# Moving the second half projections to score step 7 and two VectorE steps by one maximum in a fused transformer block

## The chip, the cores and the metric

The kernel runs on one core of a Trainium2 chip. The metric is the device time of one execution in microseconds (us). The core's engines are TensorE (PE in the profile, with PEld for its weight loads), VectorE (DVE), ScalarE (ACT), GpSimd (POOL) and SyncE (SP), which here only issues transfers.

## The reference

The input is 32 samples of 512 tokens by 256 features. Each sample goes through half a feed-forward block, an attention block, and half a feed-forward block again:

```
x = x + 0.5 * ffn(layernorm(x), Wr, br, W1, b1, W2, b2)      # routed: 2 of 8 experts per sample, gelu
x = x + attention(layernorm(x), Wqkv, Wo)                    # 16 heads of 16, rotary q and k, causal softmax
x = x + 0.5 * ffn(layernorm(x), Wr, br, W1, b1, W2, b2)
```

Inside the attention, q and k are rotated (`q = cos * q + rotate_half(q) * sin`), the scores are `q @ k.T / 4` with a causal mask, and the softmax over them weights v. Everything is float32 in the reference; the kernel splits float32 values into a high and a low float16 part and multiplies the parts.

## The kernel before

Three phases follow each other: the first feed-forward over all samples, the attention over all samples, the second feed-forward. The change is in the attention.

**Slots.** Each sample has 16 heads in four groups g = 0 to 3 of four heads. The attention runs in slots, one for each sample s and group g, in this order on each engine. Within a slot TensorE runs eleven score steps n = 0 to 10 ("score step 7" of the change is n = 6, the seventh). A step of it does two things: `scores(s, g, n)` makes transposed scores for the group two slots back, and `max_scores(s, g, n)` makes scores of the present group, only so that their row maxima can be taken. VectorE reduces each of those in `maxima(s, g, n)`, ScalarE makes the exponentials (`exps`, L1073) from the first kind, GpSimd masks the diagonals (L912), and TensorE multiplies with v (`probs_v`, L1202).

**Work between the steps.** Other work is put behind the steps by hand. On TensorE: while g is 0 or 1 the q and k projections of the next sample in four tiles t, two a slot, each as two halves of three matmuls (`project_qk`, L1219), in slot 2 its v projections (`project_v`, L1233), the transposes of a group's output (`turn_output`, L1255), and in slot 3 the transposes of the sample after the next and the output projection (`transpose_o` L1271, `project_o` L1280). On VectorE: `begin_rope` (L974 and L975) multiplies a finished q or k tile by the cosines and swaps its pairs, `rope_low` (L981) makes the low float16 part of a rotated tile, `normalise_output` (L1016, L1020) divides by the softmax sums, and `layernorm_stats` (L107 to L119) makes the statistics of the sample after the next. GpSimd finishes the rotation in `rope` (L920, L924), which begins when VectorE has swapped the pairs.

**Waits.** The maxima use three banks in turn, so `max_scores` step n waits until the maximum of about two or three steps before has ended: the first step of a slot for the ninth maximum of the slot before, step n = 5 for maximum n = 2, step n = 6 for maximum n = 3, n = 10 for n = 7. The `scores` steps use two banks: step n waits for the exponential of step n - 2. `begin_rope(t)` waits for the second half of the projection of tile t; the fourth mask of a slot waits for the last exponential, and the second `rope` of a slot stands behind that mask on GpSimd. On VectorE and GpSimd `rope_low` reads two tensors in SBUF, as do both halves of `rope`; of the other VectorE steps of a slot, the maxima, `begin_rope` and `normalise_output` read PSUM and at most one tensor in SBUF.

A "sample" below is the stretch of slots 0 to 3 of one s; times in it are those of the sample that begins at 1108.09 us of the profiled execution.

Of the kernel before, what the change touches and what calls it, by code (L numbers as in the profile page):

```python
# [58 lines left out]
def wait(eng, sem, value):  # L59

    if isinstance(value, int) and value <= 0:
        return
    eng.wait_ge(sem, value)
# [690 lines left out]
def attention(nc, ctx, tab, mem, src, dst, cos, sin, first):  # L754
# [44 lines left out]
    def after_first(eng):  # L799

        for i in range(3):
            eng.wait_ge(first.stored[i], 16 * len(range(i, B, 3)))

    def group(G):
        return not isinstance(G, int) or 0 <= G < B * 4

    def sample(s):
        return not isinstance(s.b, int) or 0 <= s.b < B

    def of_group(s, g, lag):  # L810

        return s + (g - lag) // 4, (g - lag) % 4

    def half_of(g):

        return g // 2, GH * (g % 2)
# [145 lines left out]
    def vector(dve):  # L962
        def start():
            nc.vector.memset(v[0], 1.0).then_inc(consts_set, 1)
            dve.wait_ge(consts_set, 1)

        def begin_rope(n, t):
            idx = 4 * n.b + t
            dve.wait_ge(qk_done, idx + 1)
            if idx == 0:  # L970
                dve.wait_ge(tables_loaded, 32)

            wait(dve, rope_done, idx - 1)
            nc.vector.tensor_tensor(by_cos[t % 2][:], x_ps[t % 2][:], cos_t[:], ALU.mult)  # L974
            nc.vector.stream_shuffle(swapped[t % 2][:], x_ps[t % 2][:], [i ^ 1 for i in range(32)]).then_inc(rope_in, 1)  # L975

        def rope_low(n, t):
            dve.wait_ge(qk_hi, 4 * n.b + t + 1)

            wait(dve, q_written if t < 2 else k_written, 32 * n.b)  # L980
            nc.vector.tensor_tensor(qk.lo[:, t, :], rotated[t % 2][:], qk.hi[:, t, :], ALU.subtract).then_inc(qk_lo, 1)  # L981

        def maxima(s, g, n):
            G = 4 * s.b + g
            dve.wait_ge(mx_done, 11 * G + n + 1)
            if G == 0 and n == 0:
                dve.wait_ge(over_done, 1)
            if n == 0:

                wait(dve, mt_done, G - 1)  # L990
            bank = mx_ps[MX_BANK[n]]
            out = mx[g % 2]
            if n < 4:
                i = 3 - n // 4
                w = (i + 1) * P
                nc.vector.tensor_tensor_reduce(out=bank[:, 0:w], in0=bank[:, 0:w], in1=over[:, T - w:T], scale=1.0, scalar=LOWEST,  # L996
                                               op0=ALU.add, op1=ALU.max, accum_out=out[:, n % 4, i:i + 1]).then_inc(max_done, 1)
                return
            if n < 8:
                o_ap, i_ap = out[:, n - 4, 2:3], bank[:, 0:3 * P]  # L1000
            elif n < 10:
                a = 2 * (n - 8)
                o_ap, i_ap = out[:, a:a + 2, 1], bank[:].rearrange("p (a n) -> p a n", a=2)
            else:
                o_ap, i_ap = out[:, :, 0], bank[:].rearrange("p (a n) -> p a n", a=4)
            nc.vector.tensor_reduce(o_ap, i_ap, AX_X, ALU.max).then_inc(max_done, 1)  # L1006


        def normalise_output(s, g):

            G = 4 * s.b + g
            os, og = of_group(s, g, 3)
            half, j = half_of(og)
            turned = pv_ps[:].rearrange("p (i a d) -> p i a d", i=NT, a=GH)
            dve.wait_ge(o_turned, G - 2)
            nc.vector.reciprocal(inverse[:].rearrange("p (i a) -> p i a", i=NT), turned[:, :, :, DH]).then_inc(inverse_done, 1)  # L1016

            wait(dve, oT_done, NC * (os.b - 1))
            dve.wait_ge(inverse_done, G - 2)
            nc.vector.tensor_tensor(  # L1020
                on[os.par][:].rearrange("p i (j q d) -> p i j q d", q=2, d=DH)[:, :, j:j + GH, half, :],
                turned[:, :, :, 0:DH],
                inverse[:].rearrange("p (i a d) -> p i a d", i=NT, d=1).broadcast_to([P, NT, GH, DH]), ALU.mult).then_inc(on_done, 1)

        def low_of(lo, hi, n, c, hi_done, lo_done):
            dve.wait_ge(hi_done, NC * n.b + c + 1)
            nc.vector.tensor_tensor(lo[:, c, :], x_ps[c][:], hi[:, c, :], ALU.subtract).then_inc(lo_done, 1)

        def slot(s, g):
            G = 4 * s.b + g  # L1030
            if G == 1:
                after_first(dve)
                nc.vector.memset(v[1], 1.0).then_inc(consts_set, 1)
            for n in range(11):
                if group(G):
                    maxima(s, g, n)
                if g in (1, 2) and sample(s + 1) and n in (0, 3):
                    rope_low(s + 1, 2 * (g - 1) + (n == 3))
                if group(G - 3) and n == 5:
                    normalise_output(s, g)  # L1040
                if g < 2 and sample(s + 1) and n in (2, 6):
                    begin_rope(s + 1, 2 * g + (n == 6))
                if g == 2 and sample(s + 2) and n == 1:
                    dve.wait_ge(x_loaded, 16 * ((s + 2).b + 1))

                    wait(dve, xn_done, NT * (s + 2).b)
                    layernorm_stats(nc, dve, stats_step, stats_done, (s + 2).b, x, stats, pair, ve)
                if g == 3 and sample(s + 2) and n in (1, 2):
                    low_of(xT.lo, xT.hi, s + 2, n - 1, xT_hi, xT_lo)
                if g == 3 and sample(s + -1) and n in (5, 7):  # L1050
                    low_of(oT.lo, oT.hi, s + -1, int(n == 7), oT_hi, oT_lo)
                if g == 3 and sample(s + -1) and n == 10:
                    add_residual(s + -1, 0)
                if g == 0 and sample(s + -2) and n == 0:
                    add_residual(s + -2, 1)

        def add_residual(n, j):
            dve.wait_ge(res_loaded[n.par], 16 * (n.half + 1))
            dve.wait_ge(o_done, 2 * n.b + j + 1)
            r = res[n.par][:, 2 * j:2 * j + 2, :]  # L1060
            nc.vector.tensor_tensor(r, x_ps[j][:].rearrange("p (t d) -> p t d", t=2), r, ALU.add).then_inc(res_done, 1)

        at = Turns()
        at.start, at.slot = start, slot
        return at
# [64 lines left out]
    def tensor(pe):  # L1130
# [155 lines left out]
        def slot(s, g, between=None):  # L1286
            G = 4 * s.b + g
            cur, run = group(G), group(G - 2)
            if G == 0:
                pe.wait_ge(first.gelu_done, 8 * B)  # L1290
            if G == 2:
                pe.wait_ge(stacks_set, 32)
                pe.wait_ge(first.out_done, 2 * B)
            if G == 6:
                pe.wait_ge(stacks_set, 64)
            before = group(G - 3)
            for n in range(11):
                if between:
                    between(n)
                if run and n < 10:  # L1300
                    scores(s, g, n)
                if cur:
                    max_scores(s, g, n)
                if n == 2 and before:
                    probs_v(s, g, 3, 1, 1)
                if n == 1 and group(G - 1):
                    turn_maxima(s, g)
                if n == 2 and before:
                    probs_v(s, g, 3, 2, 3)
                    probs_v(s, g, 3, 3, 2)  # L1310
                if n == 5 and before:
                    turn_output(s, g)
                if g < 2 and sample(s + 1) and n in (0, 1, 4, 5):
                    project_qk(s + 1, 2 * g + (n > 3), half=(n in (1, 5)))
                if g == 2 and sample(s + 1) and n in (0, 1, 4, 5):
                    project_v(s + 1, (0, 1, 4, 5).index(n))
                if g == 3 and sample(s + 2) and n == 0:
                    transposes(s + 2)
                if run and n == 8:
                    probs_v(s, g, 2, 0, 0)  # L1320
                if g == 3 and sample(s + -1) and n == 4:
                    transpose_o(s + -1, s)
                if g == 3 and sample(s + -1) and n >= 9:
                    project_o(s + -1, 2 * (n - 9))
                    project_o(s + -1, 2 * (n - 9) + 1)
# [285 lines left out]
```

## Time and profile before

| what | value |
|---|---|
| time, median of 3 runs | 2299.27 us (2298.2 to 2305.56) |
| the profiled execution's own time | 2291.23 us |
| its span, first to last instruction | 2289.5 us |
| PE busy | 2109.5 us, 92% |
| DVE busy | 1931.8 us, 84% |
| ACT busy | 1354.4 us, 59% |
| POOL busy | 1306.6 us, 57% |
| mean granted TensorE clock | 0.989 of 2.4 GHz |

The shares are averages over the three phases. What a change to the attention is worth has to be read from its slots: which wait ends last there. A start in the time-ordered view is that of the instruction itself; the numbers in square brackets are the idle time of the engine before it and what ended that.

### The profile page before, as it was taken

The page shows a single profiled execution, that of the slowest core. Times are in us where ns is not written, and L with a number is a line of the kernel's source. Part 1 is how long each engine was busy: PE and PEld are TensorE (multiplying, and loading weights), DVE is VectorE, ACT ScalarE, POOL GpSimd, SP SyncE. Part 2 cuts the span into 40 slices and gives each one's busy share as a digit, 9 for nine tenths or more (in the row PEclk, how much of TensorE's full clock was granted, in tenths as well). Part 3 has the DMA queues.
Part 4 walks back from the last instruction along what each step waited for, and adds up shares of the span by engine and source line. Part 5 has one row for each costly group of instructions (what it writes and reads, how often), then busy time and mean ns, then how long its engine had stood idle before and what let it go on. Part 6 is the DMA issues. An engine that isn't in the chain of part 4 may idle for free.

```text
span 2289.5 us, 52899 instructions
## 1 busy us (share of the span) xinstructions
PE 2109.5 (92%) x17682; PEld 1141.4 (50%) x17682; DVE 1931.8 (84%) x4485; ACT 1354.4 (59%) x2568; POOL 1306.6 (57%) x1462
## 2 busy tenths in 40 slices
PE   4999999889999999999999999999999888999999
PEld 2666666434444444444444444444444434666666
DVE  6777788788999899999989998999999865777776
ACT  3455444266667666666666676666666655445553
POOL 6666667454555455456545554554555425666664
PEclk9999999899999999999999999999999999999999
DMA  6656666444445444444444454444445423666665
GB/s 208 192 192 207 201 203 200 116 89 89 98 95 101 94 94 98 89 94 93 99 89 100 95 101 94 96 92 96 93 94 98 99 70 118 197 202 194 204 207 167
DMA packets 280391, 295.29 MB, mean 129 GB/s; under 512 B 45784, under 2 KB 263224, under 8 KB 280120
## 3 DMA queue, kind: packets, MB, share of 16 engines
q1 hardware_dynamic: 280120, 291.90, 50.3%
q8 instruction: 143, 2.34, 0.5%
q14 instruction: 128, 1.05, 0.2%
HBM read 140.08 MB, written 83.89 MB: 98 GB/s over the span
## 4 chain that ended last, share of the span: by engine, by line
PE 45%; DVE 33%; SPq 7%; issue 6%; DMA 5%; ACT 4%; DVEq 0%; ACTq 0%
PE bank L710 8%; DVE bank L996 7%; DVE at_mx L1006 7%; PE bank L728 7%; PE bank L1185 6%; PE bank L1202 6%; PE bank L1219 4%; PE bank L1280 4%; ACT probs L1073 3%; DVE turned L975 3%; DVE v_qk L981 3%; DVE turned L974 2%; DVE at_stats L107 2%; PE bank L1255 2%; PE bank L1167 2%
## 5 line engine op out<-in xcount | busy, mean ns | idle before, releaser
L1073 ACT ACTIVATE probs<-bank 128x512 f32<-128x512 f32 x1280 | 747.0, 603 | 456.9 <-PE bank L1185 447.5
L912 POOL TENSOR_SCALAR_AFFINE_SELECT probs<-probs 128x512 f32<-128x512 f32 x512 | 320.4, 638 | 661.1 <-ACT probs L1073 659.3
L1006 DVE TENSOR_REDUCE at_mx<-bank 128x1 f32<-128x384 f32 (+2 forms) x896 | 509.6, 608 | 78.5 <-PE bank L1167 77.0
L1185 PE MATMUL bank<-stacks 49*128 49x512 f16 (+3 forms) x2048 | 458.7, 302 | 71.4 <-ACT probs L1073 71.0
L996 DVE CUSTOM_DVE_ANT_0 bank<-bank,xn 128x512 f32<-128x512 f32 x512 | 351.6, 698 | 38.8 <-PE bank L1158 36.2
L1185 PEld LDWEIGHTS bank<-stacks 49*128 49x128 f16 x2048 | 136.0, 94 | 458.6 <-ACT probs L1073 334.2
L1162 PE MATMUL bank<-stacks 48*128 48x384 f16 (+2 forms) x1536 | 307.7, 275 | 22.1 <-DVE at_mx L1006 15.6
L1167 PE MATMUL bank<-mask,turn 64*128 64x128 bf16 (+2 forms) x896 | 230.7, 257 | 0.0
L1158 PE MATMUL bank<-stacks 48*128 48x512 f16 x512 | 198.5, 389 | 10.6 <-DVE at_mx L996 6.4
L924 POOL TENSOR_TENSOR turned<-turned 128x512 f32<-128x512 f32 x128 | 184.7, 1443 | 19.1 <-POOL turned L920 0.4
L628 ACT ACTIVATE turned<-bank,b1s 128x512 f32<-128x512 f32 x128 | 88.2, 689 | 181.0 <-PE bank L710 179.3
L920 POOL TENSOR_TENSOR turned<-turned,at_sin 128x512 f32<-128x512 f32 x128 | 178.8, 1397 | 27.7 <-DVE turned L975 27.7
L628 ACT ACTIVATE probs<-bank,b1s 128x512 f32<-128x512 f32 x128 | 88.1, 688 | 178.9 <-PE bank L710 177.3
L710 PE MATMUL bank<-stacks 128*128 128x512 f16 x768 | 172.9, 382 | 19.3 <-DVE stacks L568 15.5
L728 PE MATMUL bank<-stacks,v_qk 128*128 128x256 f16 x1536 | 172.7, 273 | 0.0
L1202 PE MATMUL bank<-probs,v_qk 128*32 128x512 f32 (+3 forms) x2048 | 168.6, 448 | 0.0
L1202 PE MATMUL bank<-probs,v 128*32 128x512 f32 (+3 forms) x2048 | 164.3, 439 | 0.0
L728 PEld LDWEIGHTS bank<-stacks,v_qk 128*128 128x128 f16 x1536 | 150.3, 98 | 17.3
L1162 PEld LDWEIGHTS bank<-stacks 48*128 48x128 f16 x1536 | 110.7, 94 | 52.5 <-DVE at_mx L1006 27.0
L710 PEld LDWEIGHTS bank<-stacks 128*128 128x128 f16 x768 | 73.9, 98 | 108.9 <-DVE stacks L568 19.1
L483 POOL TENSOR_TENSOR f_rstd<-f_ve,minus_half 128x4 f32<-128x4 f32 x64 | 91.1, 1424 | 59.4 <-DVE f_ve L119 59.4
L710 PE MATMUL bank<-xThi,w1hi 128*128 128x512 f16 x256 | 99.1, 387 | 25.2 <-DVE xTlo L568 10.6
(145 smaller groups left out, 4619.6 us busy)
## 6 DMA issues: line engine op xcount, KB each, us to landing
stacks<-qk_image SPq DMA_DIRECT2D x384, 128.0 KB, 4.5
qk_image<-v_qk SPq DMA_DIRECT2D x128, 256.0 KB, 3.7
stacks<-w_hi SPq DMA_DIRECT2D x192, 128.0 KB, 3.7
stacks<-w_lo SPq DMA_DIRECT2D x192, 128.0 KB, 3.8
b2s<-in_b SPq DMA_DIRECT2D x128, 128.0 KB, 3.9
after_ffn<-probs SPq DMA_DIRECT2D x32, 512.0 KB, 6.5
at_x<-after_ffn SPq DMA_DIRECT2D x32, 512.0 KB, 4.1
late_x<-after_ffn SPq DMA_DIRECT2D x32, 512.0 KB, 4.7
```

The costliest lines, as they stand in the source:

```text
L710: ins = nc.tensor.matmul(h_ps[j][:], w, v, start=(n == 0), stop=(n == 3 * NC - 1))
L728: ins = nc.tensor.matmul(y_ps[t // 2][:, t % 2, :], v, w, start=(n == 0), stop=(n == 11))
L912: nc.gpsimd.affine_select(out=ap, in_=ap, compare_op=ALU.is_ge, fill=0.0, base=0, pattern=[[0, d] for d in dims] + [[1, P]], channel_multi ...
L924: nc.gpsimd.tensor_tensor(rotated[t % 2][:], by_cos[t % 2][:], by_sin[t % 2][:], ALU.add).then_inc(rope_done, 1)
L996: nc.vector.tensor_tensor_reduce(out=bank[:, 0:w], in0=bank[:, 0:w], in1=over[:, T - w:T], scale=1.0, scalar=LOWEST, op0=ALU.add, op1=ALU. ...
L1006: nc.vector.tensor_reduce(o_ap, i_ap, AX_X, ALU.max).then_inc(max_done, 1)
L1073: nc.scalar.activation(probs[:, c, :], st_ps[c % 2][:], ACT.Exp, scale=DH ** -0.5).then_inc(exp_done, 1)
L1158: nc.tensor.matmul(bank[:, 0:w], q_stack[s.par][rows, j + n % 4, i * P:(i + 1) * P], k_stack[s.par][rows, j + n % 4, 0:w], start=True, sto ...
L1162: nc.tensor.matmul(bank[:, at * w:at * w + w], q_stack[s.par][rows, j + a, i * P:(i + 1) * P], k_stack[s.par][rows, j + a, 0:w], start=(at ...
L1167: nc.tensor.matmul(last, tab.turn[const, :], over.broadcast_to([HP, nh, P]), start=False, stop=True).then_inc(mx_done, 1)
L1185: ins = nc.tensor.matmul(bank[:, col:col + T - q0], k_stack[ss.par][rows, j + ha, kt * P:(kt + 1) * P], q_stack[ss.par][rows, j + ha, q0:T ...
L1202: ins = nc.tensor.matmul(pv_ps[32 * a:32 * a + 32, kt * P:T], v[ss.par][:, kt, head_of(sg, a), :], p, start=(kt == 0), stop=(nth == 3), ti ...
```

## The change

On TensorE the second half of the second q or k tile of slots 0 and 1, and the last v projection of slot 2, go from behind step n = 5 to behind step n = 6. On VectorE the first `rope_low` of slots 1 and 2 goes from behind maximum n = 0 to behind n = 1, and the layer statistics in slot 2 go from behind n = 1 to behind n = 2.

```
@@ vector, slot
             for n in range(11):
                 if group(G):
                     maxima(s, g, n)
-                if g in (1, 2) and sample(s + 1) and n in (0, 3):
+                if g in (1, 2) and sample(s + 1) and n in (1, 3):
                     rope_low(s + 1, 2 * (g - 1) + (n == 3))
                 if group(G - 3) and n == 5:
                     normalise_output(s, g)
                 if g < 2 and sample(s + 1) and n in (2, 6):
                     begin_rope(s + 1, 2 * g + (n == 6))
-                if g == 2 and sample(s + 2) and n == 1:
+                if g == 2 and sample(s + 2) and n == 2:
                     dve.wait_ge(x_loaded, 16 * ((s + 2).b + 1))
@@ tensor, slot
                 if n == 5 and before:
                     turn_output(s, g)
-                if g < 2 and sample(s + 1) and n in (0, 1, 4, 5):
-                    project_qk(s + 1, 2 * g + (n > 3), half=(n in (1, 5)))
-                if g == 2 and sample(s + 1) and n in (0, 1, 4, 5):
-                    project_v(s + 1, (0, 1, 4, 5).index(n))
+                if g < 2 and sample(s + 1) and n in (0, 1, 4, 6):
+                    project_qk(s + 1, 2 * g + (n > 3), half=(n in (1, 6)))
+                if g == 2 and sample(s + 1) and n in (0, 1, 4, 6):
+                    project_v(s + 1, (0, 1, 4, 6).index(n))
```

## Rows read from the trace of the kernel before

**Rows 1.** The page, part 4: the chain that ended last, by engine.

```profile
PE 45%; DVE 33%; SPq 7%; issue 6%; DMA 5%; ACT 4%; DVEq 0%; ACTq 0%
```

**Rows 2.** The chain over one sample: start us, us, what.

```profile
1115.90 0.62 DVE turned L974
...
1134.44 0.69 DVE bank L996
...
1135.24 0.33 PE bank L1162
```

**Rows 3.** Order of time, VectorE: the slow low half, first and last of 30.

```profile
489.51 1.19 DVE L981 TENSOR_TENSOR v_qk<-turned,v_qk 128x512 f16<-128x512 f32 x1
...
1795.46 1.19 DVE L981 TENSOR_TENSOR v_qk<-turned,v_qk 128x512 f16<-128x512 f32 x1
```

**Rows 4.** Order of time, TensorE, slot 0 from n = 5; then slot 3.

```profile
1113.72 0.66 PE L1255 MATMUL bank<-ident,at_o 128*128 128x128 f32 x4
1114.21 0.38 PE L1219 MATMUL bank<-at_xThi,qkv_hi 128*128 128x512 f16 x1
...
1114.96 0.33 PE L1185 MATMUL bank<-stacks 49*128 49x384 f16 x1
...
1115.18 0.32 PE L1185 MATMUL bank<-stacks 49*128 49x384 f16 x1
...
1116.09 0.28 PE L1185 MATMUL bank<-stacks 49*128 49x256 f16 x1 [0.52 <-ACT probs L1073]
...
1117.53 0.28 PE L1185 MATMUL bank<-stacks 49*128 49x256 f16 x1
...
1145.95 0.66 PE L1255 MATMUL bank<-ident,at_o 128*128 128x128 f32 x4
1146.53 0.33 PE L1185 MATMUL bank<-stacks 49*128 49x384 f16 x1
```

**Rows 5.** Order of time, VectorE, slots 0 to 3 of the same sample.

```profile
1114.78 0.42 DVE L1020 TENSOR_TENSOR on<-bank,at_inverse 128x256 f32<-128x256 f32 x1
1115.42 0.56 DVE L1006 TENSOR_REDUCE at_mx<-bank 128x1 f32<-128x384 f32 x1 [0.22 <-PE bank L1167]
...
1120.00 1.20 DVE L981 TENSOR_TENSOR v_qk<-turned,v_qk 128x512 f16<-128x512 f32 x1
...
1124.23 0.68 DVE L981 TENSOR_TENSOR v_qk<-turned,v_qk 128x512 f16<-128x512 f32 x1
...
1132.22 1.40 DVE L107 BATCH_NORM_STATS2 at_stats<-at_x 128x6 f32<-128x256 f32 x4
...
1139.92 1.29 DVE L1006 TENSOR_REDUCE at_mx<-bank 128x2 f32<-128x512 f32 x2 [0.39 <-PE bank L1167]
...
1141.96 0.70 DVE L996 CUSTOM_DVE_ANT_0 bank<-bank,xn 128x512 f32<-128x512 f32 x1
```

**Rows 6.** Order of time, GpSimd, slots 0 and 1 of the same sample.

```profile
1119.38 1.28 POOL L920 TENSOR_TENSOR turned<-turned,at_sin 128x512 f32<-128x512 f32 x1
1120.80 1.54 POOL L924 TENSOR_TENSOR turned<-turned 128x512 f32<-128x512 f32 x1
...
1124.27 1.77 POOL L920 TENSOR_TENSOR turned<-turned,at_sin 128x512 f32<-128x512 f32 x1
...
1131.11 1.72 POOL L924 TENSOR_TENSOR turned<-turned 128x512 f32<-128x512 f32 x1
```

**Rows 7.** Order of time, two close starts in the last phase, both engines.

```profile
1957.51 4.65 DVE L577 TENSOR_TENSOR v_qk<-turned,v_qk 128x512 f16<-128x512 f32 x4
...
1958.11 2.90 POOL L508 TENSOR_TENSOR turned<-x,b2q 128x1024 f32<-128x1024 f32 x1 [2.37 <-DMA out<-turned]
...
1944.13 2.44 POOL L508 TENSOR_TENSOR turned<-at_x,b2q 128x1024 f32<-128x1024 f32 x1 [0.85 <-DMA out<-turned]
1944.19 2.40 DVE L111 TENSOR_TENSOR f_pair<-f_stats 128x4 f32<-128x4 f32 x1
```

**Rows 8.** Order of time, TensorE: the first maximum step of slot 3.

```profile
1140.17 0.38 PE L1158 MATMUL bank<-stacks 48*128 48x512 f16 x1
```

More of the change, by code:

```diff
@@ L1036, in slot @@
                     maxima(s, g, n)
-                if g in (1, 2) and sample(s + 1) and n in (0, 3):
+                if g in (1, 2) and sample(s + 1) and n in (1, 3):
                     rope_low(s + 1, 2 * (g - 1) + (n == 3))
@@ L1042, in slot @@
                     begin_rope(s + 1, 2 * g + (n == 6))
-                if g == 2 and sample(s + 2) and n == 1:
+                if g == 2 and sample(s + 2) and n == 2:
                     dve.wait_ge(x_loaded, 16 * ((s + 2).b + 1))
@@ L1312, in slot @@
                     turn_output(s, g)
[L1313 to L1316, printed above, removed]
+                if g < 2 and sample(s + 1) and n in (0, 1, 4, 6):
+                    project_qk(s + 1, 2 * g + (n > 3), half=(n in (1, 6)))
+                if g == 2 and sample(s + 1) and n in (0, 1, 4, 6):
+                    project_v(s + 1, (0, 1, 4, 6).index(n))
                 if g == 3 and sample(s + 2) and n == 0:
```

## The prediction

> **What bounds the kernel now.** I read the page's chain first: TensorE carries 45% of what ended last and VectorE 33% [rows 1], so neither can be taken as the bound everywhere. The chain over one sample shows where it changes hands. From the start of a sample it runs on TensorE; at the end of step n = 6 of slot 0 it passes to VectorE (the first of [rows 2]), stays there through slot 1 into slot 2, and goes back to TensorE when maximum n = 2 of slot 2 has ended (its last two). Then TensorE, with links over ScalarE's exponentials, holds it until the next sample. A sample takes 45.03 us: the first slow low half starts at 489.51, the thirtieth at 1795.46, 29 periods later [rows 3]. So the change has thirty times the same effect, and I work out one sample.
>
> **VectorE and GpSimd block each other.** The first low half of slot 1 takes 1.20 us, the next one 0.68 [rows 5]. It starts at 1120.00, while GpSimd's L920 runs from 1119.38 to 1120.66, and ends 0.54 after that. The other way round, the L920 at 1124.27 takes 1.77 instead of 1.28, because the low half of 1124.23 was 0.04 ahead [rows 5, 6]. Each reads two tensors in SBUF, and the one that comes second waits for the whole of the first. The blocked low half costs 1.20 - 0.68 = 0.52 us on the chain, in each sample [rows 3]. The Trainium skill says the same ("SBUF — State Buffer", Who interferes with whom): issue order, not the operation's shape, decides who blocks. That rule speaks against any forecast that takes the moved low half at its free 0.68 without asking what GpSimd is doing at its new place; that is the main question below.
>
> **The projections on TensorE.** They move 3 matmuls in slots 0 and 1 and 6 in slot 2 past one score step; no work is added. In slot 0 the old order is output transposes (1113.72), projection (1114.21), step 6 (1114.96), step 7 (1115.18), then a stop of 0.52 until 1116.09 for the exponential of step 6 [rows 4]. In the new order step 6 follows the transposes, 0.58 after their start as in slot 3, at 1114.30 [rows 4]. The projection follows 0.33 later (as L1162 in rows 2), takes 0.75 to the next step, which is then at 1115.38, and step 8 at 1115.60. The exponential needed 1.13 from step 6 to step 8 (1114.96 to 1116.09): 1115.43, so the stop is gone. From there to step 9 it is 1.44, so step 9 comes at 1117.04 instead of 1117.53: 0.49 earlier. One more change between the two kinds of matmul is in this.
>
> What is on the chain is less. VectorE's maximum n = 6 started at 1115.42 after 0.22 idle [rows 5]; it can now follow the division (1114.78 + 0.42, less the 0.08 by which a start lies before the end ahead of it: 1115.12). So VectorE gains 0.30, no more. The rotation behind it waits for the projection, whose last matmul ends 0.32 before step 7, near 1115.44, with the maximum over at 1115.60: hidden, by 0.15 only. If that cover fails it costs the difference. In slot 1 VectorE is behind TensorE by more, so this part alone is worth nothing more there.
>
> **The first low half.** It now stands behind maximum n = 1, a further 0.61 later, so it asks at 1120.00 - 0.30 + 0.61 = 1120.31. GpSimd's L920 has ended by then (1119.38 - 0.49 + 1.28 = 1120.17), and its L924, which starts 1.42 after L920, asks at 1120.80 - 0.49 = 1120.31. That is a tie, within the 0.05 that my intervals are good for. What decides ties: in the last phase the second of the four operations that start at 1957.51 comes at 1958.11, GpSimd's L508 at 1958.11 too, and it was GpSimd's that took 2.90 against 2.44, while with GpSimd at 1944.13 and VectorE at 1944.19 it was VectorE's tiny operation that took 2.40 [rows 7]. VectorE won at a difference of 0.00, at 0.04 as well, and lost at 0.06 behind. I take it that VectorE is first.
>
> Then VectorE has gained 0.30 + 0.52 = 0.82 when slot 1's third maximum starts. This lead doesn't last. In slot 2 the first low half stands at the place that was 1132.22 - 0.61 = 1131.61, less 0.82: 1130.79. GpSimd's L924 there started at 1131.11, just behind the old low half [rows 6]; it follows TensorE's ninth step of slot 1 and comes 0.5 to 0.7 earlier, 1130.41 to 1130.61, so it is first. Free it takes 1.28, so it ends between 1131.69 and 1131.89, and VectorE goes on 0.46 later (as 1120.66 to 1121.12), at 1132.15 to 1132.35, where it used to begin the statistics at 1132.22 [rows 5]. So this collision takes the lead back: VectorE stands between 0.07 ahead and 0.13 behind. Below nothing and above nothing are both kept.
>
> **The statistics.** They take 1134.44 - 1132.22 = 2.22 us, the maximum n = 2 waited behind them, and step 5 of TensorE started its maximum matmul at 1135.24 because of it [rows 2, 5]. Behind n = 2 they no longer hold step 5; step 6 now waits for maximum n = 3, over at 1135.83 (two of 0.61 after 1134.44, and 0.17 for the read of the accumulator), so it comes at 1135.88. Then, by the intervals of slot 0: projection 1136.21, step 7 1136.96, step 8 1137.18, step 9 1138.62, step 10 about 0.4 later. VectorE's maxima, which nothing starves any more, set the rest: maximum n = 8 ended 0.39 before 1139.92, at 1139.53 [rows 5], and slot 3 begins with it at 1139.58 instead of 1140.17 [rows 8]. The distance from there to maximum n = 1 of slot 3 (1141.96) is TensorE's, so that maximum and all behind it come 0.59 earlier. The three maxima of VectorE between (0.6 each from 1139.45) reach only 1141.26. GpSimd starts the normalisation when the statistics have ended, near 1135.1, and had to finish a mask first before; its result is wanted at 1139.9 and was ready after some 3.4 us, so 0.6 later costs nothing. SyncE's queue is passed by no step: its image transfers wait for the second low half of each slot.
>
> **Sum.** 0.59, with between +0.07 and -0.13 for the collision: 0.46 to 0.66, I take 0.59. Times 30: 17.7 us. The profiled execution took 2291.23 and would take 2273.5; it is 8 us below the median of the runs, from which I take off the same: 2299.3 - 17.7 = 2281.6. Its own range is 2277 to 2287.
>
> **Rivals.** *GpSimd first at the tie* (the slower side). It decides from a few hundredths of a microsecond. L924 then runs 1120.31 to 1121.59 and VectorE goes on at 1122.05 against 1121.73 (0.61 after 1121.12) before: its lead of 0.30 has become -0.32. The second low half of slot 1 asks at 1124.55; GpSimd's L920, at 1124.27 before and now up to 0.3 earlier, is then ahead, and blocks it until near 1125.4, 0.7 more: -1.0. The next one in slot 2 loses up to 0.1. With 0.59 for the statistics a sample gets 0.4 to 0.5 longer, times 30 is 12 to 15: about 2313. For it: the tie, and that the rule of the skill (whoever issues first) gives nothing at a difference of 0. Against it: the 0.00 that VectorE won. *The samples differ*, or the collision in slot 1 costs a little and the second isn't reached: gains and losses mix, within 7 us of 2299. Against it: the thirty samples agree to 0.02. *The projection is late*: the rotation waits in slots 0 and 1, and the gain of slot 0 goes; 0.3 in the place where the second collision levels it anyway, so about 2284 still; it is in the range. *Nothing comes through*: the k and q transfers or ScalarE's exponentials hold slot 3 where the maxima did, 2299. The chain shows neither within 0.5 us there, so little.
>
> **Chances.** Forecast (VectorE first) 0.63; GpSimd first 0.20; mixed or nothing 0.17, of which a third is still faster by more. Within 0.3% is 6.9 us, about what a measurement of this kernel tells from no change. Faster 0.68, same 0.12, slower 0.20. The range: the forecast's own 2277 to 2287 holds about 0.55; to leave out no more than 0.2 it has to reach 2275 below and, over the mixed cases, the middle of the first rival, 2312.
>
> **What will show it.** The first low half of slot 1 at 0.69 and the L924 beside it near 1.8: VectorE was first. The low half of slot 2 then at 1.4 to 1.6 in place of 0.69. If instead the first is at 1.9, the first rival holds, and the second one shows 1.4. No idle time of TensorE for ScalarE at step 8 of slots 0 to 2, no wait before L1162 at step 5 of slot 2. The period would be 44.4 us, or 45.5 in the rival. I would be wrong most simply by the order of two starts that I can't tell apart by less than their error.

## The result and the profile after

The changed kernel is slower: 2316.91 us (median of 12 runs, 2309.11 to 2330.55) against 2295.80 for the kernel before on the same chips. The ratio on record is 1.0099 (the two medians alone give 1.0092), 95% interval 1.0073 to 1.0124. The forecast was 2281.6; the first rival, GpSimd first at the tie, had 2313. The profiled execution took 2312.31 us, of which this is the page.

```profile
span 2310.6 us, 52899 instructions
PE 2148.8 (93%) x17682; PEld 1141.9 (49%) x17682; DVE 1968.9 (85%) x4485; ACT 1354.3 (59%) x2568; POOL 1286.7 (56%) x1462
...
PE 49%; DVE 29%; issue 7%; SPq 6%; DMA 5%; ACT 3%; DVEq 0%; ACTq 0%
...
L981 DVE TENSOR_TENSOR v_qk<-turned,v_qk 128x512 f16<-128x512 f32 x128 | 137.7, 1076 | 0.0
```

The number of instructions is that of before. The low halves (L981) took 1076 ns on average, and a free one takes 0.69 us. Here are low halves of three samples that follow each other, in order of time on VectorE (free ones are left out but for the first; the line of L111 is one of the statistics).

```profile
1035.82 0.69 DVE L981 TENSOR_TENSOR v_qk<-turned,v_qk 128x512 f16<-128x512 f32 x1
...
1046.32 1.42 DVE L981 TENSOR_TENSOR v_qk<-turned,v_qk 128x512 f16<-128x512 f32 x1
...
1080.49 1.82 DVE L981 TENSOR_TENSOR v_qk<-turned,v_qk 128x512 f16<-128x512 f32 x1
...
1084.71 1.39 DVE L981 TENSOR_TENSOR v_qk<-turned,v_qk 128x512 f16<-128x512 f32 x1
...
1092.84 1.02 DVE L981 TENSOR_TENSOR v_qk<-turned,v_qk 128x512 f16<-128x512 f32 x1
...
1095.82 0.62 DVE L111 TENSOR_TENSOR at_pair<-at_stats 128x4 f32<-128x4 f32 x1
...
1127.24 1.81 DVE L981 TENSOR_TENSOR v_qk<-turned,v_qk 128x512 f16<-128x512 f32 x1
```

And GpSimd in the same stretches.

```profile
1034.38 1.28 POOL L920 TENSOR_TENSOR turned<-turned,at_sin 128x512 f32<-128x512 f32 x1
1035.81 1.84 POOL L924 TENSOR_TENSOR turned<-turned 128x512 f32<-128x512 f32 x1
...
1045.93 1.27 POOL L924 TENSOR_TENSOR turned<-turned 128x512 f32<-128x512 f32 x1
...
1080.48 1.28 POOL L924 TENSOR_TENSOR turned<-turned 128x512 f32<-128x512 f32 x1
...
1084.28 1.27 POOL L920 TENSOR_TENSOR turned<-turned,at_sin 128x512 f32<-128x512 f32 x1 [0.21 <-DVE turned L975]
...
1092.04 1.27 POOL L924 TENSOR_TENSOR turned<-turned 128x512 f32<-128x512 f32 x1
...
1095.79 0.64 POOL L912 TENSOR_SCALAR_AFFINE_SELECT probs<-probs 128x512 f32<-128x512 f32 x1 [2.48 <-ACT probs L1073]
```

The tie is there to the last digit of the view. "First" below means: served first, so that the other one is the slow one. At 1035.82 the low half and L924 start 0.01 apart, VectorE is first, and it is L924 that takes 1.84. At 1080.49 they are 0.01 apart again, GpSimd is first, and the low half takes 1.82. In one and the same execution both orders occur: of the last 30 samples, 18 have the low half at 1.81 and 12 at 0.69 (in the first two of the 12, at 487.39 and 531.90, L924 starts 0.05 behind, so they are no ties). From the start of one such low half to the next it is mostly 44.67 us after a sample with VectorE first (1035.82 to 1080.49) and mostly 46.51 after one with GpSimd first (1080.49 to 1127.24 has 46.75), against 45.03 before [rows 3].

Three samples take longer for another reason: 46.30 after VectorE first (from 896.52), 48.12 and 47.16 after GpSimd first (from 1266.80 and 1726.18). In each of them TensorE's granted clock is at the lower of its two levels for some 3.4 us, which no sample of the kernel before has. In the twelve runs of the changed kernel the three with the lowest mean granted clock (0.975 to 0.982) took 2326 to 2331 us, the other nine (0.984 to 0.988) 2309 to 2321.

18 times 1.48 less 12 times 0.36 is 22 us, and the spans differ by 21.1. That these agree so well is partly luck: the three samples at the lower clock add 3.9 us, and the stretches before and behind the 30 samples are some 5 us shorter than in the kernel before.

### The profile page after: what moved, and what is told of

Same layout as the page of the kernel before. It is cut to its first block, busy times and chain, and to the rows that moved or that the text cites. A ratio compares the mean times of both kernels' runs of the same rounds, so it can differ in the third digit from the quotient of the medians.

```text
span 2310.6 us, 52899 instructions
## 1 busy us (share of the span) xinstructions
PE 2148.8 (93%) x17682; PEld 1141.9 (49%) x17682; DVE 1968.9 (85%) x4485; ACT 1354.3 (59%) x2568; POOL 1286.7 (56%) x1462
## 4 chain that ended last, share of the span: by engine, by line
PE 49%; DVE 29%; issue 7%; SPq 6%; DMA 5%; ACT 3%; DVEq 0%; ACTq 0%
PE bank L710 8%; DVE bank L996 8%; PE bank L728 7%; PE bank L1185 7%; PE bank L1202 7%; DVE at_mx L1006 5%; PE bank L1219 5%; PE bank L1280 4%; ACT probs L1073 2%; PE bank L1162 2%; PE bank L1167 2%; DVE v_qk L981 2%; DVE turned L975 2%; DVE at_stats L107 2%; DMA late_x<-in_x 1%
## 5 line engine op out<-in xcount | busy, mean ns | idle before, releaser
L912 POOL TENSOR_SCALAR_AFFINE_SELECT probs<-probs 128x512 f32<-128x512 f32 x512 | 324.7, 646 | 676.0 <-ACT probs L1073 675.5
L1162 PE MATMUL bank<-stacks 48*128 48x384 f16 (+2 forms) x1536 | 316.3, 277 | 44.3 <-DVE at_mx L996 22.3
L924 POOL TENSOR_TENSOR turned<-turned 128x512 f32<-128x512 f32 x128 | 174.8, 1366 | 19.1 <-POOL turned L920 0.4
L920 POOL TENSOR_TENSOR turned<-turned,at_sin 128x512 f32<-128x512 f32 x128 | 163.4, 1277 | 31.1 <-DVE turned L975 31.1
L981 DVE TENSOR_TENSOR v_qk<-turned,v_qk 128x512 f16<-128x512 f32 x128 | 137.7, 1076 | 0.0
```

What stands on the lines that cost most here:

```text
L912: nc.gpsimd.affine_select(out=ap, in_=ap, compare_op=ALU.is_ge, fill=0.0, base=0, pattern=[[0, d] for d in dims] + [[1, P]], channel_multi ...
L1162: nc.tensor.matmul(bank[:, at * w:at * w + w], q_stack[s.par][rows, j + a, i * P:(i + 1) * P], k_stack[s.par][rows, j + a, 0:w], start=(at ...
```

## The experiments

Ten kernels, each compared with the kernel before on the same chip. The first two move nothing but the tie. To the changed kernel one memset of 128x1 is added for each sample, on VectorE or on GpSimd, into a tile that nothing reads.

**vector_late**

```
                 if g in (1, 2) and sample(s + 1) and n in (1, 3):
+                    if g == 1 and n == 1:
+                        nc.vector.memset(spare[:], 0.0)
                     rope_low(s + 1, 2 * (g - 1) + (n == 3))
```

> The changed kernel with one tiny memset more on VectorE before the first low half of slot 1, so that this low half asks some 0.1 us later. Order theory (whoever of VectorE's low half and GpSimd's L924 starts first blocks the other): GpSimd is first in all 30 samples, each low half of slot 1 takes about 1.7 to 1.8 us, every sample takes about 46.5 us, and the time is 12 samples x 1.84 = 20 us above the changed kernel's, about 2335. Rival (the step order on TensorE costs the time, the mix of 44.7 and 46.5 us samples has another cause): the mix stays, 2317.

Measured: 2339.86 us, ratio 1.0216 (1.0182 to 1.0250). From 576.36 on every first low half of slot 1, 28 of 30, is at 1.80 to 1.82, and most samples take 46.51 or 46.52. Three take 48.12 or 48.13 and two 47.17 and 46.87; four of these five have the lower clock for some 3.4 us. The time is 23 us above the changed kernel's. The mix is gone. On VectorE, then on GpSimd:

```profile
1041.51 1.81 DVE L982 TENSOR_TENSOR v_qk<-turned,v_qk 128x512 f16<-128x512 f32 x1
1041.59 0.06 DVE L1040 MEMSET at_spare<- 128x1 f32 x1
```

```profile
1041.49 1.28 POOL L925 TENSOR_TENSOR turned<-turned 128x512 f32<-128x512 f32 x1
```

The memset stands ahead of the low half in the program, but in the view the low half's start comes before it. So the reported start of this low half is not the moment at which it takes or loses its turn; the two reported starts are still only 0.02 apart.

**gpsimd_late**

```
             if g < 2 and sample(s + 1):
+                if g == 0:
+                    nc.gpsimd.memset(spare[:], 0.0)
                 rope(s + 1, 2 * g + 1)
```

> The changed kernel with one tiny memset more on GpSimd before the second rotation of slot 0, so that its L924 asks 0.1 us or more later. Order theory: VectorE is first in all samples, the low half of slot 1 takes 0.69 everywhere, every sample takes about 44.7 us, and the time is about 10 us below that of the kernel before (2285). Rival: the mix stays, 2317.

Measured: 2280.87 us, ratio 0.9959 (0.9940 to 0.9978). Order of time on GpSimd, one sample:

```profile
1067.65 0.10 POOL L959 MEMSET at_spare<- 128x1 f32 x1
1067.71 1.27 POOL L921 TENSOR_TENSOR turned<-turned,at_sin 128x512 f32<-128x512 f32 x1
1069.13 1.82 POOL L925 TENSOR_TENSOR turned<-turned 128x512 f32<-128x512 f32 x1
```

The memset puts the next operation back by 0.06 us. VectorE's low half starts at 1069.11, 0.02 ahead, takes 0.69, and does so in all 30 samples; most of them take 44.67 to 44.70. So 0.06 us of work added to GpSimd, or as little to VectorE, sets the two kernels 59 us apart (2339.9 and 2280.9), with the same steps in the same order otherwise: 51 us of it are 28 samples at 1.82 each, and about 4 come from samples at the lower clock. The order theory holds. That my 2281.6 is near this kernel's time is luck: on its chip the kernel before took 2290.78, so the gain is 10 us and not the 17.7 that I had worked out.

**The parts alone.** Each is the kernel before with one part, or two, of the diff.

```
projections_alone:            the two TensorE hunks only (n in (0, 1, 4, 6))
low_half_alone:               rope_low at n in (1, 3) only
statistics_alone:             layernorm_stats at n == 2 only
projections_and_statistics:   both, rope_low stays at n in (0, 3)
```

> Only the first low half of slots 1 and 2 is moved. It asks 0.61 later than before, 0.19 ahead of L924 (1120.80), so VectorE is first, the low half of slot 1 takes 0.69 and gains 0.52. In slot 2 it asks within 0.1 of L924 (a tie again): 44.5 us a sample if VectorE is first, 45.4 or more if GpSimd is. Rival (the moved low half is what costs by itself, through ScalarE or the image transfers): over 45.5 with both low halves at 0.69.

Measured: 2274.94 us, ratio 0.9930 (0.9904 to 0.9955), every low half at 0.68 or 0.69, 44.56 us a sample. The low half by itself is a gain. L924 starts 0.15 behind it in slot 1 and 0.09 behind it in slot 2, and VectorE is first in both. It is the projections' 0.30 and 0.49, unequal on the two engines, that bring it to the tie in slot 1.

> Only the statistics are moved. No low half changes its place against GpSimd's rotation, so slot 1 stays as before (first low half 1.20, the rest 0.69). TensorE no longer stops at step 5 of slot 2; its product of the probabilities with v then waits for the division, 0.32 earlier than before. 44.7 us a sample, or up to 45.2 if a mask of GpSimd blocks one of the small operations of the statistics, which now come 0.61 later. Rival (my forecast): 0.59 less, 44.4.

Measured: 2293.46 us, ratio 1.0024 (1.0005 to 1.0042), 45.15 us a sample: 0.12 more than before, with slot 1 as before. This is why, on VectorE and then on GpSimd:

```profile
1171.46 0.62 DVE L115 TENSOR_SCALAR at_ve<-at_pair 128x4 f32<-128x4 f32 x1
```

```profile
1171.42 0.64 POOL L912 TENSOR_SCALAR_AFFINE_SELECT probs<-probs 128x512 f32<-128x512 f32 x1 [1.78 <-ACT probs L1073]
```

An operation on 128x4 elements, 0.17 before, takes 0.62: the mask started 0.04 ahead of it and blocks it. 0.45 lost and 0.32 gained by the earlier division make 0.13. So moving the statistics past one maximum is worth nothing here, for a reason that the prediction had listed nowhere.

> The low halves stay behind the first maximum; projections and statistics are moved. Order theory: as with the projections alone, 44.2 us a sample if VectorE is first in slot 2 and 45.3 if not; the statistics add nothing, because the division on VectorE holds the probabilities' first product with v anyway (on the chain of the changed kernel). Rival (my forecast's sum, 0.59 a sample from the statistics): up to 43.9.

Measured: 2299.23 us, ratio 1.0044 (1.0030 to 1.0058). The tie in slot 2 falls to GpSimd in all samples but one: the low half there takes 1.67 and a sample 45.23, as expected for that order (three samples, at the lower clock for some 3.4 us, take 46.85). In the one sample with VectorE first it was 44.70, 0.5 above what I expected: its L115 took 0.62, blocked by the mask as above. The rival's 43.9 is out.

> Only the projections are moved. Order theory: VectorE leads by 0.33 after slot 0, the low half of slot 1 still runs into L920 but GpSimd is 0.49 earlier, so the lead is 0.49 in slot 1. In slot 2 the low half and L924 come within 0.1 of each other: if VectorE is first the sample is 44.2 us (time about -24 us), if GpSimd is first 45.3 (+8). Rival (the further switch between kinds of matmul, or the late projection holding the rotation, is what costs): a sample takes over 45.5 whatever the low halves show.

Measured: 2336.63 us, ratio 1.0218 (1.0189 to 1.0247), far more than I expected. One sample of the thirty has VectorE first in slot 2 and takes 44.24, as expected. The others have the low half at 1.67 and take about 45.7 or 47.05, about every third the first of these (one takes 48.61). Neither is 45.3. In the statistics GpSimd's mask costs 0.44 in all of them (L111 at 0.62 or 0.63), which gives 45.7. The other 1.35 goes with TensorE's clock: of the 28 samples whose length can be read, the 18 of 46.99 or more all have it at the lower level for 3.4 us or more, and the ten of 45.92 or less never have. These are two such samples by stretches, each from step 5 of slot 2 on, with the granted clock behind the counts (1.00 and 0.66):

```profile
595.30:599.10 3.80, 3.71 (x33) 1.67 (x33) 3.70 (x10) 1.91 (x5) 3.52 (x6) 1.00 1.14 151
640.99:644.80 3.81, 3.81 (x25) 1.92 (x25) 3.62 (x9) 1.08 (x2) 2.98 (x5) 0.66 1.15 154
```

And TensorE in order of time in the second one:

```profile
638.69 0.27 PE L1233 MATMUL bank<-qkv_hi,at_xTlo 128*128 128x256 f16 x1
638.80 0.27 PE L1233 MATMUL bank<-qkv_lo,at_xThi 128*128 128x256 f16 x1
...
640.99 0.33 PE L1162 MATMUL bank<-stacks 48*128 48x384 f16 x1 [1.60 <-DVE at_mx L996]
...
642.42 0.42 PE L1233 MATMUL bank<-qkv_hi,at_xTlo 128*128 128x256 f16 x1
642.63 0.42 PE L1233 MATMUL bank<-qkv_lo,at_xThi 128*128 128x256 f16 x1
```

TensorE stood for 1.60 us at step 5 (1.59 in the first of the two), waiting for the maximum behind the blocked low half and the blocked statistics. 1.2 us after it went on, its matmuls follow each other at 0.21 us in place of 0.11: the lower of its two levels, 1.2 GHz. So the rival of this run (the projections themselves cost) isn't needed: the sample with VectorE first is the fastest of the run, with the projections moved in it as in the others.

**Taking the second collision away.** The changed kernel with the first low half moved in slot 1 alone, without and with the memset on GpSimd, and then with the statistics back at their old place as well.

```
only_slot1_low, and only_slot1_low_gpsimd_late with the memset of gpsimd_late:
-                if g in (1, 2) and sample(s + 1) and n in (1, 3):
+                if g in (1, 2) and sample(s + 1) and n in (2 - g, 3):
statistics_back, on top of only_slot1_low_gpsimd_late:
-                if g == 2 and sample(s + 2) and n == 2:
+                if g == 2 and sample(s + 2) and n == 1:
```

> The changed kernel, but the first low half of slot 2 stays behind the first maximum. The tie in slot 1 is untouched: samples with VectorE first and samples with GpSimd first are mixed. With VectorE first its lead of 0.82 should now pass slot 2, since the low half there asks 0.2 ahead of L924: 43.9 us a sample, 44.3 if a mask blocks the statistics; with GpSimd first 46 to 46.5. Between 2275 and 2310 by how many fall on which side.

Measured: 2331.27 us, ratio 1.0186 (1.0157 to 1.0216): the mix again, 44.33 for a sample with VectorE first and 46.7 for one with GpSimd first. In its trace 9 samples are of the first kind and 21 of the second, more of the latter than my range allowed for.

> As the kernel before this one, with the tiny memset on GpSimd that lets VectorE be first in slot 1. All 30 samples alike, low halves 0.69 in slots 1 and 2: 43.9 us a sample (34 us faster than the kernel before, about 2257), or 44.3 (22 us faster) if a mask blocks the statistics. Rival (the collision in slot 2 was not what took the lead back): 44.7 as with the memset alone.

Measured: 2270.15 us, ratio 0.9911 (0.9889 to 0.9933), 44.33 us a sample, nearly all low halves at 0.68 or 0.69, L115 at 0.62. The lower of my two numbers is out, the one with the mask is exact.

> Projections moved, first low half moved in slot 1 alone, memset on GpSimd, and the statistics back behind the second maximum. In the kernel before this one the mask L912 blocked the statistics' L115 for 0.45 in each sample; at the old place the statistics are over before that mask asks. VectorE's lead of 0.82 plus the 0.32 that the product with v gains by following the division at once: 1.14 less than before, 43.9 us a sample, 34 us faster than the kernel before (about 2256). Rival (the statistics' move is worth something besides): not below 44.3.

Measured: 2259.18 us, ratio 0.9869 (0.9845 to 0.9893), 43.88 us a sample. On VectorE:

```profile
1147.00 0.68 DVE L984 TENSOR_TENSOR v_qk<-turned,v_qk 128x512 f16<-128x512 f32 x1
...
1156.85 0.69 DVE L984 TENSOR_TENSOR v_qk<-turned,v_qk 128x512 f16<-128x512 f32 x1
...
1159.85 0.17 DVE L115 TENSOR_SCALAR at_ve<-at_pair 128x4 f32<-128x4 f32 x1
```

The mask asks at 1160.46, when the statistics are over. This version beats both kernels, by 31 us the one before. It stands on a thin margin, though: its L925 starts only 0.01 to 0.02 behind the low half of slot 1.

**division_ahead** tests the other half of the missed size: what holds slot 3 when no low half is late. It is gpsimd_late with one low half moved.

```
-                if g in (1, 2) and sample(s + 1) and n in (1, 3):
-                    rope_low(s + 1, 2 * (g - 1) + (n == 3))
+                if g in (1, 2) and sample(s + 1) and n in (1, 3 if g == 1 else 6):
+                    rope_low(s + 1, 2 * (g - 1) + (n > 1))
```

> The changed kernel with the memset on GpSimd, and in slot 2 the second low half behind the seventh maximum, so that the division stands 0.6 earlier. If the division holds the product with v at the end of slot 2, TensorE's wait of 0.19 before it goes and a sample takes 44.5 instead of 44.7. Rival (the maxima hold slot 3, as I forecast): 44.7, no change.

Measured: 44.58 us a sample in place of 44.69 (2272.35 us, one run). Between the two: the low half at its new place took 0.85 in place of 0.69. TensorE's product (1081.36) no longer waits for the division, so the division was on the chain. In this version the next limit lies little more than 0.1 behind it; how far it would lie with a free low half is not shown.

## Why the prediction was wrong

**The step that failed** is "I take it that VectorE is first". The times of the tie were right: I had 1120.31 for both, and the trace has them 0.01 apart. The two close starts of [rows 7] did not justify a side, though: a difference of 0.00 between two rows that are rounded to 0.01, and of 0.06, leave the point of decision open by more than the samples need. What the runs showed in its place is a mix, 18 samples with GpSimd first and 12 with VectorE first. I gave the mix a sixth and expected it within 7 us of 2299.

**What sorts the samples.** The view rounds to 0.01, and there samples with 0.01 between the starts go both ways. Read to the nanosecond in the trace, the two outcomes separate. In the ten tied samples with VectorE first, L924's start is 7 to 9 ns ahead of the low half's; in the 18 with GpSimd first it is 11 to 24 ns ahead. The other traces agree: in only_slot1_low 5 to 11 ns against 13 to 19, in vector_late 15 to 26 with GpSimd first in all 28, and in the four kernels with the memset on GpSimd, where L925 starts behind the low half, VectorE first throughout. The pair of [rows 7] fits: L508's start was 8 ns ahead, and VectorE was first. So by reported starts the order turned over where GpSimd's was about 11 ns (0.011 us) ahead, and the samples of the changed kernel lie on both sides of that. A forecast from rows could not have told them apart.

**TensorE's part was right.** Slot 0 ahead of the low half of 1035.82 (VectorE first) reads:

```profile
1029.21 0.66 PE L1255 MATMUL bank<-ident,at_o 128*128 128x128 f32 x4
...
1029.80 0.33 PE L1185 MATMUL bank<-stacks 49*128 49x384 f16 x1
...
1030.12 0.39 PE L1219 MATMUL bank<-at_xThi,qkv_hi 128*128 128x512 f16 x1
...
1031.11 0.27 PE L1185 MATMUL bank<-stacks 49*128 49x256 f16 x1
...
1032.54 0.28 PE L1185 MATMUL bank<-stacks 49*128 49x256 f16 x1
```

From the output transposes to step 9 it is 3.33 us (1032.54 less 1029.21), 3.81 before [rows 4]: 0.48 earlier, forecast 0.49. The stop before step 8 is gone. VectorE's maximum n = 6 follows the division without a gap (1030.60 behind 1030.26 and 0.42), as forecast.

**The first low half, VectorE first:** forecast 0.69 with L924 near 1.8, then 1.4 to 1.6 in slot 2 and the lead of 0.82 given back. The rows show 0.69, 1.84 and 1.42. Right.

**The statistics, 0.59 forecast, 0.36 measured** per sample with VectorE first. I had let only the maxima limit what follows step 8. The product of the probabilities with v at step 8 also waits for `normalise_output`, which reads the bank that the product writes (the wait on `on_done`). The chain of the changed kernel, VectorE to TensorE:

```profile
1053.04 0.44 DVE on L1020
...
1053.52 1.07 PE bank L1202 x8
```

Here the product starts 0.48 after the division's start. Before, the division was over in time (it started at 1137.58, the product at 1138.38), so by the same 0.48 it could give back 0.32, not 0.59. The wait stands in the code and I did not read it. Thirty times the difference is 7 us: gpsimd_late's samples gain 10 in place of 17.7, and the rest up to its measured time against the 2299 that I started from is the spread between chips and runs.

**The rival's price, 0.4 to 0.5 a sample forecast, 1.48 measured.** Its two losses in slot 1 were right: 1.02 together, with L981 at 1.82 and 1.39 (forecast 1.0). In slot 2 I had up to 0.1 for the low half; it was 0.33 (L981 took 1.02 in place of 0.69), because the late division of slot 1 also holds TensorE's product there, and behind it step 9 and with it L924 (this row is of the sample from 1266.80, also one with GpSimd first):

```profile
1274.07 1.06 PE L1202 MATMUL bank<-probs,v 128*32 128x512 f32 x8 [0.19 <-DVE on L1020]
```

The mask blocks L111 for 0.45 (0.62 in place of 0.17, at 1095.82, with L912 at 1095.79), which I had not looked for. 1.02 + 0.33 + 0.45 is 1.80, and that much later the division of slot 2 comes; less the 0.32 that it can give back it is 1.48, as measured.

That the rival's 2313 lies near the measured 2316.91 is luck. It had all 30 samples at 0.4 to 0.5; the runs have 18 at 1.48 and 12 that gain.

**The small operations.** L111 (two inputs in SBUF) and L115 (one) work on 128x4 elements, and a mask of GpSimd held either for 0.45. [rows 7] already had such a case: an L111 of 128x4 took 2.40 beside GpSimd's L508. The prediction used it for the order of two starts and did not ask the same of the statistics. The Trainium skill ("SBUF — State Buffer", Who interferes with whom) says that a VectorE operation with two inputs in SBUF contends with a GpSimd operation that reads it, and that tensor_scalar can contend by its two-port mode. The traces agree that both were blocked (L111 0.62, L115 0.62, each 0.17 when free); whether L115 was in that mode no run shows.

Still open: the runs don't tell where the spread of some 10 ns between the samples comes from, what the chip goes by at the moment of decision, and why of two stops of the same length only one is followed by the low clock.

## What to carry to other kernels

Where two engines block each other whole, a step's place in the order isn't its cost: put the start of each operation that can be blocked, small ones too, beside the other engine's list at the new place, and move it only to where some tenths of a microsecond lie between. A computed tie in a loop that repeats can come out as a mix, and the sum is then as uncertain as the price of the worse side. Of the versions here low_half_alone was 0.7% faster with 0.15 and 0.09 us between the starts and no memset; the fastest one, statistics_back, depends on 0.01 to 0.02 us. And before a gain is counted through a chain of steps, list every wait of each step on it, also those that never showed idle time before.

## What the runs showed of the hardware

- 0.06 us of work on one engine or the other set the whole program 59 us apart (gpsimd_late against vector_late), mostly through 28 collisions decided one way or the other.
- By reported starts, the order of VectorE's low half and GpSimd's second rotation step turned over where GpSimd's start was about 0.011 us ahead (the changed kernel and only_slot1_low).
- VectorE's operations on 128x4 elements are blocked by a mask on GpSimd for 0.45 us, both with two inputs in SBUF (L111) and with one (L115, tensor_scalar).
- In projections_alone TensorE stood for 1.60 us, and the granted clock was 0.66 over the next 3.8 us in one sample; in the sample before it, after a stop of 1.59, it was 1.00. The low clock cost that sample 1.35 us. The changed kernel has it in three samples: one takes 48.12 in place of 46.51, with 0.74 granted over 6.3 us (1286.6 to 1292.9) behind a stop of 0.71 that ended at 1284.15. A stop of that length is in nearly all of its samples, and in the third of the three the low clock came behind idle times of 0.26 and 0.19 only.
